# One fused 16-sequence kernel: an order of its own for the head and the first two periods of the last loop

## The reference

```python
x = x + LN(attention(LN(x)))      # 16 heads, rotary positions, causal
x = x + LN(moe0(LN(x)))           # 16 experts, top 2 of a softmax, 2 shared ones
x = x + LN(ssm(LN(x)))            # state-space layer, 8 heads of 64, state 16
x = x + LN(moe1(LN(x)))           # 16 experts, top 8 of a sigmoid, 2 shared ones

# ssm, for each sequence:
gate, xBC, dt = split(LN(x) @ W_in)
xBC = silu(conv(xBC, 4 taps))     # over time
dt  = softplus(dt + dt_bias);  dA = exp(-dt * exp(A_log))
h_t = h_(t-1) * dA_t + (dt_t * x_t) B_t^T;   y_t = h_t C_t + D_skip * x_t
out = rmsnorm(y * silu(gate)) * norm_w @ W_out

# moe1, for each token, with comb = normalised top-8 weights times 2.5, all experts computed:
out = sum_e comb[e] * (silu(h @ Wg[e]) * (h @ Wu[e])) @ Wd[e]  +  shared
```

## Time and profile before

| | us |
|---|---|
| median of 3 runs (1949.41 to 1953.84) | 1953.65 |
| the profiled execution | 1951.19 |
| its span | 1949.2 |
| TensorE busy in the span | 1837.1 (94%) |
| VectorE busy | 1265.4 (65%) |
| ScalarE busy | 766.9 (39%) |
| GpSimd busy | 423.3 (22%) |

### The profile page before, as it was taken

One profiled execution on the slowest core, in us unless ns is written; L12 is line 12 of the kernel. 1 busy time (PEld: TensorE's weight loads), 2 busy tenths in 40 slices (PEclk: granted clock), 3 DMA queues, 4 the chain that ended last, 5 costly groups with the idle time before them and its releaser, 6 DMA issues.

```text
span 1949.2 us, 33656 instructions
## 1 busy us (share of the span) xinstructions
PE 1837.1 (94%) x9995; PEld 1422.1 (73%) x10013; DVE 1265.4 (65%) x3638; ACT 766.9 (39%) x1483; POOL 423.3 (22%) x708
## 2 busy tenths in 40 slices
PE   7999999969989999777999999999999999999998
PEld 5566666547766666555888888888888888888886
DVE  4677777636422222377777877787787778877843
ACT  2566666532223333343343343334333433433321
POOL 1343444322854444200110011001001100110000
PEclk7999999959989999887999999999999999999999
DMA  9900000001323332342202211220222022102110
GB/s 351 225 13 1 0 0 1 1 1 44 117 101 94 93 95 93 126 147 82 73 16 88 82 44 48 87 82 18 75 87 82 6 87 82 59 33 71 66 50 11
DMA packets 92135, 137.87 MB, mean 71 GB/s; under 512 B 18564, under 2 KB 76164, under 8 KB 91524
## 3 DMA queue, kind: packets, MB, share of 16 engines
q1 hardware_dynamic: 85124, 117.83, 18.9%
q0 software_dynamic: 6912, 18.92, 2.7%
HBM read 98.51 MB, written 38.22 MB: 70 GB/s over the span
## 4 chain that ended last, share of the span: by engine, by line
PE 44%; issue 38%; DVE 8%; POOL 5%; ACT 2%; DMA 1%; DVEq 0%; POOLq 0%; another core or an unknown queue 0%; ACTq 0%; SPq 0%
PE bank L610 6%; PE bank L184 5%; PE bank L1314 4%; PE bank L631 4%; PE bank L1379 3%; PE bank L193 2%; PE bank L1272 2%; PE bank L1320 2%; PE bank L1407 2%; PE bank L1302 2%; PE bank L559 1%; POOL sorted_in L858 1%; PE bank L621 1%; PE bank L1365 1%; PE bank L539 1%
## 5 line engine op out<-in xcount | busy, mean ns | idle before, releaser
L184 PE MATMUL bank<-moe_xT,up_w 128*128 128x256 f32 x2304 | 545.6, 380 | 0.0
L184 PEld LDWEIGHTS bank<-moe_xT,up_w 128*128 128x128 f32 x2304 | 438.6, 190 | 59.9
L227 ACT ACTIVATE moe_silu<-bank 128x256 f32<-128x256 f32 x288 | 110.4, 383 | 574.3 <-PE bank L184 574.3
L193 PE MATMUL bank<-down_w,moe_hT 128*128 128x256 f32 x1152 | 303.9, 387 | 5.6 <-DVE moe_hT L294 2.8
L193 PEld LDWEIGHTS bank<-down_w,moe_hT 128*128 128x128 f32 x1152 | 207.1, 190 | 39.1 <-DVE moe_hT L294 7.9
L1565 DVE TENSOR_REDUCE q_slots<-bank 128x4 f32<-128x1024 f32 (+1 forms) x96 | 117.7, 1226 | 76.6 <-PE bank L1314 76.0
L1466 ACT ACTIVATE probs<-bank 128x1024 f32<-128x1024 f32 x96 | 98.1, 1022 | 101.2 <-PE bank L1320 101.2
L610 PE MATMUL bank<-up_w,moe_xT 128*128 x320 | 116.9, 488 | 0.7 <-ACT moe_xT L676 0.6
L830 DVE TENSOR_TENSOR moe_h<-moe_silu,bank 128x176 f32<-128x176 f32 x80 | 27.0, 337 | 138.2 <-issue 86.0
L1314 PE MATMUL bank<-kT,qT 16*128 16x256 f32 (+1 forms) x1024 | 114.3, 351 | 0.0
L1320 PE MATMUL bank<-qmT,kT 17*128 17x512 f32 x384 | 113.2, 663 | 0.8 <-ACT probs L1466 0.8
(11 more groups left out here) (310 smaller groups left out, 3217.1 us busy)
## 6 DMA issues: line engine op xcount, KB each, us to landing
up_w<-comb_rows SPq DMA_DIRECT2D x32, 768.0 KB, 5.2
m<-decay_rows SPq DMA_DIRECT2D x16, 1024.0 KB, 5.0
comb_got<-results SPq DMA_DIRECT2D x16, 768.0 KB, 7.8
moe_rows<-sorted_in SPq DMA_DIRECT2D x80, 128.5 KB
sorted_in<-zero SPq DMA_DIRECT2D x10, 1024.0 KB, 10.1
...
up_w<-in_up SPq DMA_DIRECT2D x2, 2304.0 KB, 12.1
```

The costliest lines, as they stand in the source:

```text
L184: last = mm(k.bank[:, UP_BANK + i % 3, half * S:(half + 1) * S], m.w_up[:, c, at + half * m.inter:at + (half + 1) * m.inter], m.xT[:, par, ...
L193: last = mm(k.bank[:, SUM_BANK, j * D:(j + 1) * D], m.hT[:, i % 3, j * P:(j + 1) * P], m.w_down[:, m.expert(i), :], start=(i == 0 and j == ...
L227: nc.scalar.activation(m.silu[:, i % 3, :], k.bank[:, UP_BANK + i % 3, 0:S], ACT.Silu).then_inc(m.silu_ready, 1)
```

## The change

1. The head's order is changed: the projection and `dt` steps of sequence 0 stand together and the `l_up` of b behind them. `turn_dA`, `decay_out`, `decay_in` come ahead of both `gate` steps. ScalarE's part of `l_up` becomes a step of its own, `l_silu`, so that it can stand elsewhere than the matmuls.
2. Period 0 gets its own list, `FIRST`: the `dt` chain and the dA transposition of sequence 1 run to their end there before its `gate` and `conv`; `post` and the routing of sequence 0 come ahead of `conv` 1 to 3 of sequence 1; experts 0 to 2 of sequence 0 stand right behind `m_turn`, and `down` 0 with them.
3. Period 1 gets its own list, `SECOND`, with 15 experts instead of 18. The combining and normalising of sequence 2, which stood in period 0, is here, beside that of sequence 3.
4. `scale_w_out` takes the product of `w_out` and `norm_w` out of `ssm_vector` and puts it behind the sparse stage's shared steps, ahead of its blocks.
5. Waits follow the new order: `m_turn` of sequence 0 waits for the gates of sequence 1, `m_turn_c` of sequence 0 for its own `m_exp`, `turn_x` of sequences 1 and 2 and the first `turn_c` of sequence 1 for other readers of the shared bank.

```diff
@@ scale_w_out, called in sparse_vector behind the shared steps
+def scale_w_out(k, m, dve):
+    dve.wait_ge(m.loaded, m.LOADS)
+    for f in range(FT):
+        last = k.nc.vector.tensor_scalar(m.w_out[:, f, :], m.w_out[:, f, :], m.norm_w[:, f:f + 1], None, ALU.mult)
+    last.then_inc(m.w_out_ready, 1)
@@ moe_tensor
         if what == "m_turn":
             pe.wait_ge(m.xn_ready, t + 1)
-            if not isinstance(t, int) or t + 1 < SEQS:
+            if isinstance(t, int) and t == 0:
+                pe.wait_ge(ssm.gate_ready, 4)
+            elif not isinstance(t, int) or t + 1 < SEQS:
                 pe.wait_ge(ssm.xtok_ready, 2 * t + 4)
...
         if what == "m_turn_c":
-            if not isinstance(t, int) or t + 2 < SEQS:
+            if not isinstance(t, int) or 0 < t and t + 2 < SEQS:
                 pe.wait_ge(ssm.xT_ready, t + 3)
@@ Tail
+    FIRST = (
+        ("gmat", 0, 0), ("scan", 0, 0), ("weight", 0, 0), ("c_fetch", 2, 0),
...
+        ("gate", 1, 0), ("conv", 1, 0), ("post", 0, 0), ("gate", 1, 1), ("post", 0, 1), ("m_norm", 0, 0), ("m_norm", 0, 1),
+        ("m_turn", 0, 0), ("m_logits", 0, 0), ("m_exp", 0, 0), ("l_end", B, 0), ("conv", 1, 1),
+        ("up", 0, 0), ("m_route", 0, 0), ("m_turn_c", 0, 0), ("comb_out", 0, 0), ("comb_in", 0, 0), ("comb_in", 0, 1),
+        ("conv", 1, 2), ("up", 0, 1), ("h", 0, 0), ("conv", 1, 3), ("silu", 1, 0),
+        ("up", 0, 2), ("h", 0, 1), ("down", 0, 0), ("turn_c", 1, 0), ("turn_c", 1, 1),
+    )
+    SECOND = (
+        (("gmat", 1, 0), ("scan", 1, 0), ("weight", 1, 0), ("xdt", 1, 0)),
+        (("scan", 1, 1), ("weight", 1, 1), ("comb_in", 0, 2)),
+        (("scan", 1, 2), ("weight", 1, 2)),
+        (("ymm", 1, 0), ("scan", 1, 3), ("weight", 1, 3), ("c_sum", 2, 0)),
+        (("gating", 1, 0), ("ymm", 1, 1), ("square", 1, 0), ("c_sum", 2, 1)),
+        (("gating", 1, 1), ("square", 1, 1), ("c_norm", 2, 0), ("norm", 2, 0)),
+        (("out", 1, 0), ("norm", 2, 1), ("turn_x", 2, 0), ("c_fetch", 3, 0)),
...
+        (("m_norm", 1, 1), ("turn_dt", 2, 0), ("dt", 2, 0), ("conv", 2, 0)),
+        (("gate", 2, 0), ("conv", 2, 1), ("table", 2, 0), ("one_plus", 2, 0), ("table", 2, 1), ("c_sum", 3, 0)),
+        (("gate", 2, 1), ("conv", 2, 2), ("dt", 2, 1), ("conv", 2, 3), ("c_sum", 3, 1), ("silu", 2, 0)),
+        (("turn_c", 2, 0), ("turn_c", 2, 1), ("dt", 2, 2), ("c_norm", 3, 0), ("m_turn", 1, 0), ("norm", 3, 0),
+         ("m_logits", 1, 0), ("table", 2, 2), ("m_exp", 1, 0), ("norm", 3, 1), ("turn_dA", 2, 0), ("decay_out", 2, 0)),
+        (("turn_x", 3, 0), ("m_route", 1, 0), ("decay_in", 2, 0), ("m_turn_c", 1, 0), ("comb_out", 1, 0), ("xdt", 2, 0),
+         ("comb_in", 1, 0), ("comb_in", 1, 1)),
+    )
@@ Tail.head
-        yield from self.period(0, 0)
-        yield "l_end", B, 0, 0
-        yield from self.period(1, 1)
+        for what, t, i in self.FIRST:
+            yield what, t, t % 2, i
+        for n, then in enumerate(self.SECOND, 3):
+            for what, t, i in (("up", 0, n), *then, ("h", 0, n - 1), ("down", 0, n - self.LAG)):
+                yield what, t, t % 2, i
```

More of the change, by code:

```diff
@@ L903, in sparse_sync @@
     go_through(m.blocks, sp, block)
[L906 removed]
+LATE_STEPS = ("l_norm", "l_turn", "l_up", "l_silu", "l_h", "l_down", "l_end")
 class Late:
@@ L2168, in ssm_vector @@
     dve.wait_ge(m.loaded, m.LOADS)
-    for f in range(FT):
-        last = ts(m.w_out[:, f, :], m.w_out[:, f, :], m.norm_w[:, f:f + 1], None, ALU.mult)
-    last.then_inc(m.w_out_ready, 1)
     ts(m.a_lim[:], m.a_log[:], 88.0, None, ALU.min).then_inc(m.log_ready, 1)
@@ L2330 @@
     )
+    FIRST = (
+        ("gmat", 0, 0), ("scan", 0, 0), ("weight", 0, 0), ("c_fetch", 2, 0),
+        ("feat", 1, 0), ("scan", 0, 1), ("weight", 0, 1), ("feat", 1, 1), ("scan", 0, 2), ("weight", 0, 2),
+        ("ymm", 0, 0), ("scan", 0, 3), ("weight", 0, 3), ("bcdt", 1, 0), ("gating", 0, 0), ("turn_dt", 1, 0), ("ymm", 0, 1),
+        ("square", 0, 0), ("dt", 1, 0), ("table", 1, 0), ("gating", 0, 1), ("square", 0, 1), ("one_plus", 1, 0), ("table", 1, 1),
+        ("out", 0, 0), ("dt", 1, 1), ("dt", 1, 2), ("table", 1, 2), ("turn_dA", 1, 0), ("decay_out", 1, 0), ("decay_in", 1, 0),
+        ("gate", 1, 0), ("conv", 1, 0), ("post", 0, 0), ("gate", 1, 1), ("post", 0, 1), ("m_norm", 0, 0), ("m_norm", 0, 1),
[4 more added lines that the diff above has]
+    )
```

33 lines of the change are left out of this document (20 added, 13 removed).

## The result

| | before | changed |
|---|---|---|
| median, runs side by side, us | 1953.08 (7 runs) | 1959.26 (1956.84 to 1964.05, 7 runs) |
| ratio, 95% interval | | 1.0049 (1.0027 to 1.0071) |
| the profiled execution / its span, us | 1951.19 / 1949.2 | 1961.73 / 1960.0 |
| period 2 starts at, us | 965.80 | 976.60 |

The change makes the kernel slower, by 0.3% to 0.5%: the two medians divide to 1.0032, the ratio on record is 1.0049, and its interval excludes 1. The page's first lines after (span; then the busy times) say that the work is the same: VectorE, ScalarE and GpSimd have the counts of before. TensorE has 17 records more (10012 for 9995), 16 of them matmuls of the attention stage that the trace of before lacks (48 for 64). The 10.8 us more of span are exactly the 10.8 by which period 2 starts later.

A forecast was written before the change was run, and what follows sets the result against it. TensorE was taken to set the time from period 1 on; 15.3 us gained up to `up` 3 is lost again, net +4.7: 1951.19 + 4.7 = 1955.9, and half of the median's 2.5 offset gives 1957, range 1946 to 1965.

The forecast's parts named there:

- second rival: Period 1: both TensorE pauses bring the lower clock, VectorE holds up period 2's start; +6 to +12, 1959 to 1965, chance 0.25.
- likeliest case: End of period 1: early experts are paid back, period 2 starts 1 to 8 us later; 1952 to 1962, chance 0.53.
- The forecast's own mechanism: Period 1: the 15.3 us gained up to up 3 is paid back by its end, period 2 starting 4.7 later.
- w_out: Start of the tail on VectorE: four products moved into the sparse stage's wait, what follows 1.25 us earlier.
- Head: Head of the tail: first scan 1.65 us earlier, at 854.7; a 9.5 us earlier m goes unused.
- FIRST: Period 0: post at 875.2, first up at 885.9, up 3 at 896.75 instead of 912.07, a gain of 15.3 us.
- SECOND, steps 3 to 7: Early period 1: first weight waits for gmat to 899.4, second ymm at 916.1, TensorE idle 4.7 us in all.
- Steps 7 to 13: Middle of period 1: TensorE has all the work, 26 us without a gap, to turn_dt at 942.1.
- Steps 13 to 17: End of period 1: VectorE has all the work, 25.2 us to 967.2; period 2 at 968.4 before the clock's part.
- The clock: End of period 1: after TensorE's idle 953.7 to 958.1, short steps run at 1.2 GHz; period 2 from 968.4 to 970.5.
- The upper bound: Period 2's start at most +9: a clock fall also at 916 adds 1.7, VectorE stalls at two crossings (one expert, 2.6).
- the signs named: Trace marks from first scan to period 2's first up, including TensorE pauses of about 3 and 4 to 5 us.

The follow-up runs named there:

- e1: The kernel before with only the w_out product moved into the sparse stage; D, tail's first VectorE instruction to period 2's first up, 157.3 (before 158.4); one run, 1947.59 us.
- e8: The changed kernel with gmat, scan 0 and weight 0 of sequence 1 moved from behind up 3 to ahead of both turn_c; ratio to before 1.0029.
- e3: The changed kernel with matmuls of no use filling TensorE's pauses of period 1, no wait changed; ratio to before 1.0020.

## Why the prediction came out as it did

The sum gave 1955.9 for the profiled execution, 4.7 above before; it took 1961.73, 10.5 above. The forecast for the median was 1957, the measured one is 1959.26, inside the likeliest case's range (1952 to 1962) and the wide one (1946 to 1965). Part of that nearness is luck: the text put the median above the profiled execution, and it came 2.5 below it, which hides more than half of the miss. By mechanism the first half of the second rival came true, *slower by the clock* (+6 to +12): both pauses brought the lower level. Its other half did not: VectorE's first scan of period 2 did wait 0.64 for `m`, at 976.37, but the last wait on TensorE's path to the `up` at 976.60 was one for ScalarE. The forecast's own mechanism, the lead paid back at the end of period 1, is what the rows show; the price of the clock in it was too low.

- *w_out.* Taken at 1.25; e1 shows 1.5 at the first scan and 1.1 in D. Right.
- *Head.* First scan predicted at 854.7, measured 854.62 (with the tail's start 0.2 later). The head's own order was worth some 0.4, as much as the walk gave it (1.65 less 1.25), and the 9.5 us "not used" were not used.
- *FIRST.* `post` predicted at 875.2, measured 875.04 (884.10 before); router input ready at 882.2, measured 881.82 (881.09 + 0.73); `m_route` 886.2, measured 884.78; `up` 3 896.75, measured 895.38. The gain was 16.7, not 15.3: the first `up` ran at full clock (1.97), the case that the text named.
- *SECOND, steps 3 to 7.* Weight 0 waits until 899.4, measured 899.80; second `ymm` 916.1, measured 916.59. The times are right, by two misses that cancel: `up` 3 started 1.4 earlier than predicted and ran at the lower level (3.53), a fall of the clock that the walk has nowhere. Nor did the walk say what it was worth to avoid the wait: three steps in another place, in the 6 us in which VectorE waited, take back 7.0 in the trace of e8.
- *Steps 7 to 13.* 26 us predicted from the second `ymm` to `turn_dt`, without a gap. There was none, but it took 28.6, and 25.7 in e3, at full clock. So `turn_dt` came at 945.18 instead of 942.1, for which the 0.5 of the `ymm` and 2.9 of the clock behind the first pause account.
- *Steps 13 to 17.* 25.2 us of VectorE to the end of the route, measured 26.1 (945.51 to 971.6). The order of the waits, for the first tap (1.57), for `s_e` (1.79), for the exp of the route (1.09), was the predicted one.
- *The clock* is the term that was mis-sized. Predicted: 2.1 us, at the second pause alone, and 1.7 more only as a bound. Measured by e3: 2.9 behind the first pause and 3.9 at the second, 6.8 in all. Of the 3.9 the short steps make up only 1.6 (from the first `turn_c` to `turn_dA` 7.2 in after, 5.7 in e3); the rest lies in `turn_dA`, `down` 14 (1.91) and `up` 17 (3.23), which ran at the lower level too. With 6.8 in place of 2.1 that accounts for 4.7 of the 6.1 missing; another 0.5 is the `ymm`.
- *A wait that the walk missed.* `m_turn_c` waits for ScalarE's copy of `turn_x` of sequence 3, which stands right ahead of it: 0.77 at 975.52, on TensorE's path to period 2, in e3 as well. With this the sum is 4.7 + 4.7 + 0.5 + 0.8 = 10.7, closer to the 10.8 than its terms are known.
- *The upper bound.* +9 is 4.7 + 1.7 + one stall of 2.6. With a stall at each of the two crossings, as the text has it, it would be +11.6, and the measured 10.8 lies between.

The table loads came out as the rows said: in the profile after, a load starts at 950.49 and the exp behind it at 951.78, 1.29 later.

```profile
950.49 1.28 ACT L1993 ACT_TABLE_LOAD   x1
...
951.78 0.22 ACT L1993 ACTIVATE s_e<-s_mn 128x16 f32<-128x16 f32 x1
```

By the Trainium skill ("ScalarE: Activation LUTs", What ACT_TABLE_LOAD costs) a drain of 1.38 us comes on top of the load at every switch to another set. Here, as in the rows of before, none shows: the activation ahead of the load ends at 950.47, 0.02 before it.

Of the signs named, the pause ahead of the second `ymm` (2.90), the one ahead of `turn_c` (4.30, by the silu), VectorE's 5.95 ahead of `s_u`, the granted clock of 0.50 (from 961 to 967) and the first `up` at 884.13 were found. `up` 3 came 1.6 before the 897 named. Period 2's first `up` at 968 to 971 was not found.
